# A score stage whose pieces get their rest from an accumulating transfer instead of a subtraction

## The reference

```python
def _lap_mul(A, x):
    d = 1.0 / jnp.sqrt(jnp.sum(A, axis=-1))
    return d[:, None] * (A @ (d[:, None] * x))
z = _lap_mul(A, x) @ W1 + b1
z = jax.nn.leaky_relu(z, negative_slope=0.1)
sq = jnp.sum(z * z, axis=-1)
d2 = jnp.maximum(sq[:, None] + sq[None, :] - 2.0 * (z @ z.T), 0.0)
S = jnp.exp(-jnp.sqrt(d2 + 1e-10) / 2.0)
ranks = jnp.argsort(jnp.argsort(-S, axis=-1), axis=-1)
A2 = jnp.where(ranks < 4, S, 0.0) + A
out = _lap_mul(A2, x) @ W2 + b2
return _layernorm(x + out, axis=-1)
```

## Time and profile before

| | us |
|---|---|
| median of 3 runs | 2698.08 (2696.41 to 2700.05) |
| the profiled execution | 2700.21 |
| its span, first to last instruction | 2698.3 |

### The profile page before, as it was taken

The page is one execution under the profiler, slowest core; times in us unless marked ns, Lnnn a source line. Parts: engine busy times, 40 slices in busy tenths (PEclk is TensorE's granted clock), DMA queues, the critical chain, the costliest instruction groups (busy, mean ns, idle before and its releaser), DMA issues.

```text
span 2698.3 us, 29101 instructions
## 1 busy us (share of the span) xinstructions
PE 2455.5 (91%) x9356; PEld 1708.8 (63%) x9356; DVE 2319.3 (86%) x1411; ACT 1609.8 (60%) x1911; POOL 1190.0 (44%) x981
## 2 busy tenths in 40 slices
PE   0367999999999999799999999999999998899998
PEld 0133444444577777577778787877778775566765
DVE  7998889977788887999999998989999877487886
ACT  0000000000376776899998998989898884477775
POOL 0000000000000000167778787887888896777771
PEclk9778999999999999999999999999999999999999
DMA  9999999997699980035555454545555569999995
GB/s 382 421 398 414 393 420 421 421 420 274 255 368 344 341 313 32 1 122 183 152 148 162 151 160 143 167 143 162 155 154 157 163 188 341 396 401 396 391 378 214
DMA packets 147917, 718.18 MB, mean 266 GB/s; under 512 B 19024, under 2 KB 26960, under 8 KB 86608
## 3 DMA queue, kind: packets, MB, share of 16 engines
q1 hardware_dynamic: 124384, 670.49, 65.9%
q0 software_dynamic: 18800, 37.77, 5.6%
q10 hardware_dynamic: 4608, 8.39, 0.8%
HBM read 680.40 MB, written 36.18 MB: 266 GB/s over the span
## 4 chain that ended last, share of the span: by engine, by line
PE 55%; ACT 12%; DVE 11%; issue 9%; DMA 9%; POOL 3%; SPq 0%; ACTq 0%; POOLq 0%; DVEq 0%
PE PS L754 19%; ACT R L1123 5%; PE PS L853 4%; PE PS L855 4%; PE PS L854 4%; DMA ring<-at 4%; PE PS L821 3%; DVE R L1601 3%; PE PS L894 3%; PE PS L953 2%; PE PS L895 2%; DVE R L1604 2%; PE PS L904 2%; PE PS L817 2%; PE PS L818 2%
## 5 line engine op out<-in xcount | busy, mean ns | idle before, releaser
L1281 POOL TENSOR_TENSOR al<-ring,ah 128x1024 fp32r<-128x1024 f32 x264 | 637.2, 2418 | 195.0 <-ACT ah L1094 185.4
L1601 DVE MAX8 R<-R 128x8 f32<-128x8192 f32 x64 | 555.8, 8685 | 78.4 <-ACT R L1123 78.1
L1123 ACT ACTIVATE R<-PS 128x1024 f32<-128x1024 f32 x512 | 519.5, 1018 | 119.3 <-PE PS L861 76.0
L1604 DVE FIND_INDEX8 R<-R,R 128x8 uint32<-128x8192 f32 x64 | 555.8, 8685 | 0.3 <-issue 0.3
L1254 POOL CAST zst<-zh 128x128 fp32r<-128x128 f32 (+1 forms) x64 | 24.8, 387 | 1122.2 <-DVE zl L1536 811.7
L853 PE MATMUL PS<-zh,zst 128*128 128x512 f32 x1024 | 408.0, 398 | 40.8 <-ACT R L1123 22.2
L855 PE MATMUL PS<-zh,zst 128*128 128x512 f32 x1024 | 399.8, 390 | 0.0
L854 PE MATMUL PS<-zl,zst 128*128 128x512 f32 x1024 | 399.8, 390 | 0.0
L1109 ACT ACTIVATE PS<-R 128x1024 f32<-128x1024 f32 x310 | 318.0, 1026 | 6.1
L1436 POOL DMA_INDIRECT R<-xs_dram,R x256 | 281.5, 1100 | 88.4 <-issue 76.2
L1028 ACT ACTIVATE tiny<-rowsum 128x4 f32<-128x4 f32 x16 | 3.3, 206 | 482.1 <-DVE rowsum L1471 482.1
(11 more groups left out here) (169 smaller groups left out, 4281.7 us busy)
## 6 DMA issues: line engine op xcount, KB each, us to landing
R<-at SPq DMA_DIRECT2D x152, 1024.0 KB, 11.4
ring<-at SPq DMA_DIRECT2D x148, 1024.0 KB, 9.5
ring<-at SPq DMA_DIRECT2D x264, 512.0 KB, 3.6
cache<-at SPq DMA_DIRECT2D x117, 1024.0 KB, 20.2
raw_sq<-at SPq DMA_DIRECT2D x21, 1024.0 KB, 9.6
raw_z<-at SPq DMA_DIRECT2D x20, 1024.0 KB, 9.5
raw_ring<-at SPq DMA_DIRECT2D x20, 1024.0 KB, 8.1
acc_dram<-R POOLq DMA_DIRECT2D x78, 256.0 KB, 5.7
```

The costliest lines, as they stand in the source:

```text
L1123: act.activation(score[j % 2][:, c * EC:(c + 1) * EC].rearrange("p (b c) -> p b c", b=2), pair(first, j, c), ACT.Copy).then_inc(copied, 1)
L1281: pool.tensor_tensor(al[:, k % SPLIT], raw[k % RAW], ah[:, k % SPLIT].bitcast(F32), ALU.subtract)\
L1601: v.max(top[:, j], score[j % 2]).then_inc(dve3, 1)
L1604: v.max_index(place[:, j], top[:, j], score[j % 2]).then_inc(placed, 1)
```

## The change

The rest of a piece is no longer computed by POOL from two tiles. The piece is loaded into one of CUTS = 7 buffers; POOL multiplies it in place by -1 and rounds it (`minus_rounded`), so that the buffer holds the rounded negative; PE reads that; then POOL issues a transfer of the same 512 KB of `adj` that adds it onto the buffer (`add_piece`), which leaves `a - round(a)`, the rest. PE reads the buffer a second time. Since the first read had the wrong sign, the second uses the negative of `xgh` (`nxgh`, a new tile), and ACT's flush multiplies by -1.

With it:

- ACT rounds no piece any more; POOL rounds all of them, two pieces ahead (ROUND_AHEAD).
- The second half of a piece comes 3 pieces after its first (2 in group 0), at a chunk of its own.
- SP loads piece n after the second half of piece n - 7; the three stores of a group's `xg`, `xgh`, `xgl` come after the fifth load (third before), the reload of `xg` after the eighth.
- The pieces of group 6 go into 36 chunks instead of 41, all others at the chunks that they had.
- Pieces are counted through by n instead of (g, k), and PE, ACT, POOL and SP have no loop over groups any more. POOL's waits in these parts lose the increment of `gate` ahead of them (`hold`).
- The six seeded chunks stay seeded; the order of the seeds is named by SEED_ORDER.
- `dynamic_dma_scratch_size=8192` is given to the compiler.

```diff
-RAW, SPLIT, BANKS = 3, 2, 2
+CUTS, BANKS = 7, 2
+ROUND_AHEAD = 2
-ON_POOL = tuple(k for k in range(HB * (GT // 2)) if k % 3 == 2 or 31 <= k)
...
+        cuts = [sb(f"cut{k}", [P, PT, BC], F32R, at=top_of["ring"] + k * PIECE * 4) for k in range(CUTS)]
+        raws = [sb(f"raw{k}", [P, PT, BC], at=top_of[f"cut{k}"]) for k in range(CUTS)]
+        nxgh = sb("nxgh", [P, GT, D], F32R)
...
+        def chunk_of(n):
+            g, k = group_of[n], n - pieces_before(group_of[n])
+            if g == 0:
+                return EARLY_AT + k * (2 * GT * NE + LATE_IN - EARLY_AT) // NP0
+            if g == G - 2:
+                return (g + 1) * GT * NE + 2 * NE + GAP + ((k + 1) * ((GT - 2) * NE - GAP - 5) - 1) // NP
+            if k >= early:
+                return (g + 2) * GT * NE + (2 * (k - early) + 1) * LATE_IN // (2 * late)
+            return (g + 1) * GT * NE + 2 * NE + GAP + ((k + 1) * ((GT - 2) * NE - GAP) - 1) // early
+
+        def second_chunk_of(n):
+            lag, end = (2 if n < NP0 else 3), pieces_before(group_of[n] + 1) - 1
+            return chunk_of(n + lag) if n + lag <= end else chunk_of(end) + 2 * (lag + n - end) - 1
...
+            for n in range(N_PIECES):
+                g = group_of[n]
+                if n >= CUTS:
+                    sp.wait_ge(prodb, n - CUTS + 1)
+                sp.dma_start(raws[n % CUTS][:, :, :], source_of(n)).then_inc(ld_b[n % CUTS], 16)
+                k = n - pieces_before(g) - (NP0 // 2 if g == 0 else 0)
+                if k == 4:
+                    store_group(g)
+                if k == 7:
+                    sp.wait_ge(s_xg, 16 * (g + 1))
+                    sp.dma_start(xg, x[:, (g + 1) * GT:(g + 2) * GT]).then_inc(s_xn, 16)
...
+            def second_half(n):
+                _, _, p = place_of_piece(n)
+                if group_chain(n):
+                    pe.wait_ge(nxgh_ok, group_chain(n))
+                pe.wait_ge(rest[n % CUTS], 16 * (n // CUTS + 1))
+                for kk in range(PT):
+                    i = pe.matmul(PS[:, 4 + unit(n) % BANKS], nxgh[:, p * PT + kk], cuts[n % CUTS][:, kk],
+                                  start=False, stop=closes(n) and kk == PT - 1, skip_group_check=True)
+                i.then_inc(prodb, 1)
...
-                act.activation(ah[:, k % SPLIT], raw[k % RAW], ACT.Copy).then_inc(rounded, 1)
+                act.activation(flush, PS[:, 4 + w % BANKS], ACT.Copy, scale=-1.0).then_inc(flushed, 1)
...
-                pool.tensor_tensor(al[:, k % SPLIT], raw[k % RAW], ah[:, k % SPLIT].bitcast(F32), ALU.subtract)\
-                    .then_inc(rest, 1)
+            def minus_rounded(n):
+                pool.wait_ge(ld_b[n % CUTS], 16 * (n // CUTS + 1))
+                pool.tensor_scalar(cuts[n % CUTS][:, :, :], raws[n % CUTS][:, :, :], -1.0, None, ALU.mult)\
+                    .then_inc(rounded, 1)
+
+            def add_piece(n):
+                pool.wait_ge(ah_read, n + 1)
+                pool.dma_start(cuts[n % CUTS][:, :, :], source_of(n), accum_op=ALU.add)\
+                    .then_inc(rest[n % CUTS], 16)
...
+                        for n in first_at[at_c]:
+                            if n + ROUND_AHEAD < N_PIECES:
+                                minus_rounded(n + ROUND_AHEAD)
+                            add_piece(n)
+                        if not first and (j, c) == (2, NE - 1):
+                            minus_high_of_xg(g - 1)
...
+    nc = bacc.Bacc("TRN2", target_bir_lowering=False, num_devices=1, dynamic_dma_scratch_size=8192)
```

More of the change, by code:

```diff
@@ L366, in build @@
         ah_read = sem("ah_read")
-        rounded_pool = sem("rounded_pool")
+        nxgh_ok = sem("nxgh_ok")
         s_acc = sem("s_acc")
         s_acc_in = [sem(f"s_acc_in{k}") for k in range(len(ACC_AT))]
-        ld_b = [sem(f"ld_b{s}") for s in range(RAW)]
+        ld_b = [sem(f"ld_b{s}") for s in range(CUTS)]
         prodb = sem("prodb")
@@ L376, in build @@
         rounded = sem("rounded")
-        rest = sem("rest")
+        rest = [sem(f"rest{s}") for s in range(CUTS)]
         idx_ok = sem("idx_ok")
@@ L478, in pieces_before @@
             return 0 if is_first(g) else NP * g + (NP0 - NP)
-        def following(g, k):
-            return (g, k + 1) if k + 1 < count(g) else (g + 1, 0)
-        def on_pool(g, k):
-            return k % RAW == RAW - 1 if is_first(g) else k in ON_POOL
-        def rounds(g, k):
-            return sum(on_pool(g, i) for i in range(k))
-        def rounds_before(g):
-            return 0 if is_first(g) else len(ON_POOL) * g + (rounds(0, NP0) - len(ON_POOL))
-        def act_rounds_before(g):
-            each = NP - len(ON_POOL)
-            return 0 if is_first(g) else each * g + (NP0 - rounds(0, NP0) - each)
-        def raw_turn(g, k):
-            before = 0 if is_first(g) else (NP // RAW) * g + (NP0 - NP) // RAW
-            return 16 * (before + k // RAW + 1)
-        def wait_rounded(eng, g, k):
-            if on_pool(g, k):
-                eng.wait_ge(rounded_pool, rounds_before(g) + rounds(g, k) + 1)
-            else:
-                eng.wait_ge(rounded, act_rounds_before(g) + k - rounds(g, k) + 1)
         def is_first(n):
@@ new lines, in build, with flush_chunk_of @@
+        last_of = {unit(n): n for n in range(N_PIECES)}
+        def flush_chunk_of(w):
+            return second_chunk_of(last_of[w]) + (0 if last_of[w] < NP0 else 1)
+        first_at = [[n for n in range(N_PIECES) if chunk_of(n) == at_c] for at_c in range(CHUNKS)]
+        second_at = [[n for n in range(N_PIECES) if second_chunk_of(n) == at_c] for at_c in range(CHUNKS)]
+        flush_at = [[w for w in range(UNITS) if flush_chunk_of(w) == at_c] for at_c in range(CHUNKS + 2)]
+        assert all(second_chunk_of(n) < CHUNKS for n in range(N_PIECES))
@@ L568, in is_last @@
+        assert all(second_chunk_of(n) <= second_chunk_of(n + 1) for n in range(N_PIECES - 1))
+        assert all(flush_chunk_of(w) <= chunk_of(last_of[w] + 1 + PIECES // 2 * (1 if w < 2 * len(ROWS_0) else 2))
+                   for w in range(UNITS - 2))
         def is_last(g):
             return isinstance(g, int) and g == G - 1
-        def pieces_at(g, j, c):
-            if isinstance(g, int) and (g < 3 or g == G - 1):
-                return {0: turn_0, 1: turn_1, 2: turn_2, G - 1: turn_last}[g][j][c]
-            return turn[j][c]
@@ L627, in tiles_of @@
             return bass.ds(g * GT, GT)
-        def has_next(g, back, k):
-            return not (isinstance(g, int) and g == G - 1 and back == 1 and k == NP - 1)
         @block.sync
@@ L1142, in group_act @@
                             root_of_sums(g, True)
-                        if first and (j, c) == (PRE + 2, 3):
-                            round_piece(0, 0)
-                        for back, k in pieces_at(g, j, c):
-                            if has_next(g, back, k) and not on_pool(*following(g - back, k)):
-                                round_piece(*following(g - back, k))
                         if c + 3 in SEEDED and not (first and j < PLAIN_TILES):
@@ L1411, in _ @@
             stationary(0, 0, True)
-            group_pool(0)
-            for g in (1, 2):
+            for g in range(G):
                 group_pool(g)
-            with pool.Fori(3, G - 1) as g:
-                group_pool(g)
-            group_pool(G - 1)
-            add_unit(G - 2, HB - 1)
+            for w in flush_at[CHUNKS]:
+                add_unit(w)
             for u in range(BY_POOL):
```

238 lines of the change are left out of this document (85 added, 153 removed).

## The result

The changed kernel took 2890.55 us (median of 4, 2880.22 to 2897.39) against 2698.97 for the kernel before (4 runs): a ratio of 1.0705 (1.069 to 1.0719), 192 us slower. The direction was forecast, the size was not: 2754 us with a range up to 2830. The profiled executions have spans of 2698.3 and 2892.7 us, 194.4 apart.

What follows compares the result with a forecast made beforehand. Before, PE has the least room; after, DMA time bounds the score stage: +30 us in five steady groups, +4 in the first 48 pieces, +22 in the last stretch, together +56 on 2698.1, so 2754 us, range 2668 to 2830.

Steps and rivals of the forecast that it cites:

- What bounds the kernel before: Score stage: PE has least room, 143.3 of a group's 150.9 us; PE, ACT and DVE hold one another; DMA has room.
- ACT relieved by 166 us: On ACT, 158 roundings of 1.051 us go, so its copies of scores come sooner.
- POOL: 1.09 us for a multiplication, at most 2.42: On POOL, multiplication priced by the cast, with subtraction as upper bound; 71 us a group, not on the path.
- The price of the issue: On POOL, issuing an adding transfer takes 0.873 us, twice that if a 4 KB row is written as two.
- The wait ahead of the issue, 0.9 us for each piece if not covered: On POOL, the issue waits until PE has read the rounded piece; PE's order and rounding two ahead cover it.
- DMA: 2.6 us for the adding transfer: Score stage: each adding 512 KB transfer takes 2.6 us of all engines (1.25 to 2.96), 3.85 with its plain load.
- The estimate of 2.5 us by that page: By the skill's factor of 1.93, an adding transfer is 2.5 us and the sum 27 us smaller.
- The sum, bytes of a stretch over its time: Score stage: DMA time against each stretch's time; a steady group 156.9 against 150.9 us; together +56 us.
- Rival B: Last groups: the second transfer's landing, not DMA share, delays second halves; +42 there, +20 in all, 2718 us; chance 0.09.
- the first 48 pieces: Score stage, 1152.9 to 1363.7 us: transfers take 215 us against 211, so +4.
- The last stretch, +22: From 2118.2 to 2249.9 us: 153.5 us of transfers, after 8.8 off for seven loads already in, against 131.7.
- What would show it: Profile signs: middle DMA slices 0.95 to 1.0, 290 GB/s, software queue 69%, landing 8 us, group 157 us, POOL down 30%.

Runs made afterwards that it cites:

- e4: The changed kernel with a cast on POOL in place of the multiplication by -1, so the sign is left out: 2828.63 us (1.0472).
- e5: The changed kernel with a cast on POOL and no second transfer, only the semaphore raised, so the rests are left out: 2667.18 us (0.9885).
- e13: The kernel before with three places instead of two for the rounded piece and its rest, descriptors' scratch at 4096: 2702.77 us (1.0016).
- e15: The kernel before with POOL rounding 20 of a steady group's 36 pieces instead of 15, so ACT rounds fewer: 2698.74 us (0.9991).
- e6: The changed kernel, multiplication on POOL kept, with no second transfer, only the semaphore raised, so the rests are left out: 2672.92 us (0.9907).
- e1: The changed kernel with ACT making the rounded negative and POOL only issuing the adding transfers: 2843.46 us (1.0527).
- e8: A separate kernel of transfers alone, with the same shapes and issuing engines: 1.29 us a plain piece, 2.49 us an adding one, 3.81 us a pair.
- e14: The changed kernel with POOL issuing the transfer of piece n before multiplying piece n + 2, not after: 2876.79 us (1.065).
- e2: The changed kernel with a plain second transfer instead of an adding one, so the sum is not the right one: 2756.03 us (1.0203).
- e11: The changed kernel with a cast on POOL, eight buffers, and second halves four pieces behind the first (three in the last group): 2798.23 us (1.037).
- e12: As e11, but with adding transfers only for the pieces in six of the eight buffers, other rests left out: 2774.47 us (1.0282).
- e7: The changed kernel with a cast on POOL and adding transfers only for pieces in five of seven buffers, other rests left out: 2794.89 us (1.0359).

## Why the prediction was right and wrong

The forecast was 136.5 us short of the 2890.55. With a cast on POOL, which takes the 1.04 us that I had put, the kernel takes 2828.63 (e4): 62 us of the 136.5 go with the price of the multiplication, and the other 75 stay: time that the sum of bytes does not have.

- *What bounds the kernel before.* Right as far as tried: the floor without new costs is PE at 146.5 us a group (forecast 146.1), shown by e5. What holds the kernel before at 150.9 is not shown; e13 and e15 didn't move it.
- *ACT relieved by 166 us.* Right: the group of 158 roundings is gone and its other groups are as before; the busy line falls by 121 only, because spans of ACT that overlap count once in it (the groups of the list add up to 1696 us before and 1533 after, so 163 less). It bought nothing, since ACT's copies now stand 425 us idle, 413 of them behind PE. By itself it's worth little, too: fewer roundings on ACT in the kernel before (e15) made no measurable difference.
- *POOL: 1.09 us for a multiplication, at most 2.42.* **This term failed.** It is 2.76 us at least (3.06 in the median of e6), above the upper bound. I had taken the cast as the nearest row since it has one input and the same shape, and the subtraction as a bound since it has two. The bound was no bound: with one input the multiplication takes longer than the subtraction with two. The row that was missing could not be had from the trace, and then the upper end should have been wider; I had even named "its multiplication at 2 us" as what would make me wrong. Its cost is 47 to 62 us (e1, e4 against the changed kernel), by the delay of the issue and not by POOL's own sum (6 us where nothing is issued behind it, e6). The price of the issue, 0.87 us, was right (e8).
- *The wait ahead of the issue, 0.9 us for each piece if not covered.* Understated. I asked only whether PE had read the piece. But the issue stands behind the multiplication of the piece two ahead, 2.76 us; exchanging them gave 34 us in five groups (e14).
- *DMA: 2.6 us for the adding transfer.* Right: 2.49 alone, 3.81 for the pair against 3.85. The Trainium skill ("Collectives: The Full Stack", Part 3, "The bandwidth ceiling") measures a factor of 1.93 between copying and adding on a ring between cores, and the trace agrees: 2.49 over 1.29 is 1.93. The estimate of 2.5 us by that page was nearer than my 2.6. The transfers are the larger part of the loss: 134 us by adding instead of copying, and 83 more between copying and none (e2 against e6).
- *The sum, bytes of a stretch over its time.* **This step failed too.** It took PE's waits to be nothing but the excess of bytes, and it let the loose part of a group pay for the dense one. A steady group with the measured prices is 154 us by it; e4 took 163.1. The dense part by itself, 26 x 3.81 + 6.5 x 1.3 = 107.5 us, is 11.5 more than PE's 96, so some 158 for a group. The starts of the matmuls of the first halves (L853) in the traces give the two parts, as means of four groups, from the first of the 26 pieces to the first of the 10 and on to the next 26:

| kernel | dense part: transfers by their prices | dense part measured | loose part measured |
|---|---|---|---|
| e5 | 42 | 94.2 | 52.1 |
| changed | 107.5 | 112.8 | 60.3 |
| e4 | 107.5 | 106.2 | 57.5 |
| e11 | 107.5 | 101.9 | 55.1 |
| e12 | 91 | 102.1 | 55.0 |
| e7 | 88 | 102.5 | 55.4 |

So two thirds of the loss lie in the dense part, and the loose part gives nothing back, it grows too. In e4 the dense part is as long as its transfers. But e7 and e12, whose transfers fit, are 8 us above e5 there as well, and e11 passes the same transfers as e4 in less. Bytes over the dense part are a better sum than bytes over the group; they are not the whole. What the runs show in their place, in every kernel of the first table but e1, is PE's wait for the landing or for the bank. No run moved the pieces.
- *Rival B, "in a steady group three pieces are 11 us, enough".* **Here the path was wrong.** The mechanism was the right one, and I confined it to the last groups. With the landing of 8.4 us, the issue behind a multiplication and the flush's wait, 11 us are too short in every group; the excess above the floor is this wait for the most part (table). In the first 48 pieces the distance is only two, with 39 us of such waits from 1163 to 1390 us, where I forecast +4 and +26.5 came. My chance for it was 0.09, and it stood as an alternative to the bandwidth, whereas the two work in a row: the traffic makes the landing long, and the landing makes PE wait.
- *The last stretch, +22.* It was +51. To PE's last second half it took 175.3 us (2261.4 to 2436.7), where 132.1 were taken before and 153.5 forecast; the tail, forecast to shift only, took 8 more. The bytes' sum for a tile was near (33 us against 34), but I had taken 8.8 us off for seven loads already in, which no run shows.
- *The clock.* No term of the sum had it; it was put at nothing without a reason. In the 136 us above it is 0.90 on the mean, in the same stretch of the kernel before (2118 to 2250 us) 1.00. 27 us are at 1.2 GHz, with 53 matmuls: an estimate of 11 us of the 29 that the last stretch was short, and 28 in five steady groups. These are upper ends, since PE, had it been quicker, might have waited longer for the next landing; no run separates the two.
- *What would show it.* DMA slices full: right. 290 GB/s: 242, and 257 in e4, of the 275 that the same mix makes alone. Software queue at 69%: 65.2% from 1400 to 2100. Landing of 8 us or more: 8.4. Group of 157: 174. POOL's busy time down by 30% in the stage: up, 1190 to 1451.5 over the whole.

Open: how much of e4's 16.6 us above the floor is a full DMA in the dense part and how much a landing too long for three pieces. e11 and e12 both end near 157 with a new wait for the bank, which hides what either would reach without it. A third bank, which would tell, was not tried. Nor is it shown how much of the first 48 pieces' 26.6 us is their distance of two.

## What to carry to other kernels

A transfer that takes over arithmetic is to be priced twice: by its bytes, over the densest part of the schedule rather than over its mean, and by its landing plus what stands ahead of its issue, against the time until the reader comes back. When that second sum is near the distance, every small addition on the issuing engine counts: here 1.7 us more of multiplication before each issue cost 62 us. An operation that the trace does not show has no upper bound from a neighbour that looks more expensive; leave the range open there, or find a schedule that does not depend on it.

## What the runs showed of the hardware

- On POOL a multiplication by a constant (TENSOR_SCALAR, 128x1024, float32 in, rounded float32 out) takes 2.76 us, a cast of the same tile 1.04 (1034 and 2760 ns as the smallest of 264 each, e4 and the changed kernel; the medians are 1.05 and 3.13), and the subtraction of two tiles 2.42. The multiplication of `xgh` into `nxgh`, which isn't in place, is as slow: 2.77 us in the median in e6.
- A transfer that adds onto SBUF moves 211 GB/s in rows of 4 KB, a copy 407, a factor of 1.93; both at once 275 (e8, one execution).
- The share of the DMA engines can read 0.99 at 242 GB/s (changed kernel) and 1.03 at 257 (e4), where the same mix of loads and adding transfers alone moves 275: a full share isn't a full throughput.
- Beside adding transfers a plain load of 512 KB lands in 7.1 us, against 3.6.
- After PE had stood still for 2.3 to 4.6 us the granted clock fell to 0.50 for 3.4 or 6.8 us (changed kernel, at 1401.8 and 1487.1 us), with matmuls 0.427 us apart instead of 0.227.
